# Set-up of a graph-attention kernel folded into the engines' order tables, the f2 column turned on TensorE, and a new order of all steps

## The reference

```
h  = relu(layernorm(x));  Wh = h @ W[h]                     # 4 heads, 256 -> 256
f1 = Wh . a[h, :256];  f2 = Wh . a[h, 256:]
e  = leaky(f1[n] + f2[m]), masked by adj;  attn = softmax(e)
head = elu(attn @ Wh)                                       # 4 heads side by side: 1024
out  = elu(one more such attention, W_out 1024 -> 256)      # the "BACK" head
y    = relu(out @ w1 + b1) @ w2 + b2 + out
x    = x + layernorm(y) * gamma + beta
g    = relu(layernorm(x)); Wi, Wj = halves of W
x    = x + deg * (g @ Wi.T + b) + adj @ (g @ Wj.T)
```

## Time and profile before

| | |
|---|---|
| median of 3 runs | 1505.46 us |
| the profiled execution | 1505.55 us |
| its span in the trace | 1503.5 us |
| TensorE busy | 1339.4 us, 89% |
| VectorE busy | 1190.4 us, 79% |
| ScalarE busy | 1083.5 us, 72% |
| GpSimd busy | 349.2 us, 23% |
| mean granted TensorE clock | 0.982 |

### The profile page before, as it was taken

One profiled execution on the slowest core, in us unless ns is written; L12 is line 12 of the kernel. 1 busy time (PEld: TensorE's weight loads), 2 busy tenths in 40 slices (PEclk: granted clock), 3 DMA queues, 4 the chain that ended last, 5 costly groups with the idle time before them and its releaser, 6 DMA issues.

```text
span 1503.5 us, 27090 instructions
## 1 busy us (share of the span) xinstructions
PE 1339.4 (89%) x9944; PEld 1260.0 (84%) x9944; DVE 1190.4 (79%) x2833; ACT 1083.5 (72%) x2037; POOL 349.2 (23%) x234
## 2 busy tenths in 40 slices
PE   1679898999999999999999999999999999998873
PEld 1579898888999888899988888898898999888753
DVE  6687879797988979797887979789797978968442
ACT  1577978787868778777877877687787778678431
POOL 0012123232231322223131223213122321403121
PEclk9889999999999999999999999999999999999996
DMA  4101111111101111110111111001121101101001
GB/s 169 55 22 29 22 32 34 29 36 27 50 18 29 50 29 36 37 43 15 29 50 29 47 32 36 15 29 50 29 50 29 36 15 32 34 15 36 22 20 36
DMA packets 53091, 54.07 MB, mean 36 GB/s; under 512 B 14048, under 2 KB 41696, under 8 KB 52832
## 3 DMA queue, kind: packets, MB, share of 16 engines
q1 hardware_dynamic: 52960, 52.35, 12.9%
HBM read 43.78 MB, written 8.55 MB: 35 GB/s over the span
## 4 chain that ended last, share of the span: by engine, by line
PE 51%; DVE 35%; issue 6%; ACT 5%; POOL 2%; DMA 2%; POOLq 0%; ACTq 0%; DVEq 0%; SPq 0%
PE ps L747 33%; DVE arg L625 12%; PE ps L780 5%; DVE prob_lo L606 4%; DVE arg L653 4%; PE ps L830 4%; PE ps L871 4%; PE ps L840 3%; DVE elu L661 2%; DVE zneg L633 2%; DVE whx_lo L606 2%; DVE st L587 1%; POOL hx_lo L378 1%; DVE xb L699 1%; PE ps L849 1%
## 5 line engine op out<-in xcount | busy, mean ns | idle before, releaser
L378 POOL TENSOR_TENSOR hx_lo<-elu,hx_hi 128x512 fp32r<-128x512 f32 x128 | 171.2, 1338 | 622.7 <-ACT hx_hi L474 622.7
L747 PE MATMUL ps<-prob_hi,whx_hi 128*128 128x256 f32 x1024 | 298.5, 291 | 11.4 <-DVE wk L661 7.6
L747 PE MATMUL ps<-prob_lo,whx_hi 128*128 128x256 f32 x1024 | 289.7, 283 | 0.0
L747 PE MATMUL ps<-prob_hi,whx_lo 128*128 128x256 f32 x1024 | 289.2, 282 | 0.0
L625 DVE CUSTOM_DVE_ANT_0 arg<-f2bc,mask 128x512 f32<-128x512 f32 x320 | 278.7, 907 | 1.9 <-DMA f2bc<-f_rows 1.6
L444 ACT ACTIVATE arg<-arg,nmax 128x512 f32<-128x512 f32 x320 | 227.7, 718 | 0.6 <-DVE nmax L636 0.5
L440 ACT ACTIVATE arg<-arg,fcol 128x512 f32<-128x512 f32 x320 | 213.5, 721 | 12.1 <-DVE gmax L625 12.1
L780 PE MATMUL ps<-ident,arg 128*128 128x128 f32 x1280 | 186.9, 290 | 36.9 <-DVE arg L653 32.4
L747 PEld LDWEIGHTS ps<-prob_hi,whx_hi 128*128 128x128 f32 x1024 | 196.1, 192 | 17.2 <-issue 9.7
L780 PEld LDWEIGHTS ps<-ident,arg 128*128 128x128 f32 x1280 | 170.6, 209 | 45.0 <-DVE arg L653 34.8
L450 ACT ACTIVATE prob_hi<-ps 128x1024 fp32r<-128x1024 f32 x160 | 163.4, 1021 | 58.7 <-PE ps L747 33.1
(11 more groups left out here) (126 smaller groups left out, 3142.6 us busy)
## 6 DMA issues: line engine op xcount, KB each, us to landing
f2bc<-f_rows SPq DMA_DIRECT2D x80, 256.0 KB, 3.8
xin<-in_x SPq DMA_DIRECT2D x16, 512.0 KB, 4.6
xb<-in_x SPq DMA_DIRECT2D x16, 512.0 KB, 5.0
out_x<-xb SPq DMA_DIRECT2D x16, 512.0 KB, 3.2
f_rows<-fcol SPq DMA_DIRECT2D x80, 2.0 KB, 3.4
arg<-in_adj SPq DMA_DIRECT2D x1, 1024.0 KB, 5.4
ff<-in_L_gnn_a_heads SPq DMA_DIRECT2D x1, 1024.0 KB, 9.7
ff<-in_L_gnn_W_out SPq DMA_DIRECT2D x1, 1024.0 KB, 5.6
```

The lines of the kernel that those rows point to most:

```text
L378: pool.tensor_tensor(out=hx[1][:, 2 * c.h:2 * c.h + 2, c.u * HN:(c.u + 1) * HN], in0=elu[:, c.buf, :, :], in1=hx[0][:, 2 * c.h:2 * c.h + 2 ...
L747: i = pe.matmul(out, a, b_, start=(k == 0), stop=(k == n - 1))
```

## The change

1. **Set-up in the tables.** The waits on `s_setup` and `s_hi` go. New steps are done once, for batch 0, in the tables: `wh_prep` (one head each: four dots, the split), `mask`, `gc_turn`, `wo_prep`, `adj_cast` (adj to float, deg), `adj_turn` (two chunks each), `load_wo`, `load_adj`. Each consumer has its own wait (`s_wh`, `s_mask`, `s_wo`, `s_gc_lo`, `s_adj_out`), at batch 0 only.
2. **Load order.** SP issues x of batch 0 first, then W_heads, a_heads, adj, W_gc and the rest. adj is loaded twice: once into `arg` for the mask, once more into `ff` when W_out has been used.
3. **f2 turned by TensorE.** A new step `f2turn`, five per batch: TensorE transposes the 128x4 column to 4x128 in a PSUM pair, ScalarE copies it to `f2row`, and `f2send` writes 4 pieces of 512 bytes in place of 128 of 16. The row in DRAM is then in natural order, and so are the mask and `turn_p`.
4. **New tables** for all five engines. Of TensorE 48 entries for 40 (five `f2turn`, three once-only).

The core of the diff:

```diff
+            sp.dma_start(xin[:, :, :], x_v[0]).then_inc(x_loaded, 16)
             for k in range(KC):
                 sp.dma_start(w_heads[k][:, :, :], W_heads[:, k * P:(k + 1) * P, :].rearrange("h p o -> p h o")).then_inc(ld[LD_WH], 16)
...
-                sp.dma_start(f2_rows[head % 4].rearrange("(q c) -> q c", c=NC), column, allow_slow_non_contiguous=True).then_inc(f2_out[head % 4], 16)
+                sp.wait_ge(f2_row, head + 1)
+                sp.dma_start(f2_rows[head % 4].rearrange("(c q) -> c q", c=NC), f2row[:, :]).then_inc(f2_out[head % 4], 16)
...
+            def f2row_(c):                                   # ScalarE
+                head = unit_number[c.b, c.info, 0] // 2
+                act.wait_ge(f2_turned, head + 1)
+                if head > 0:
+                    act.wait_ge(f2_out[(head - 1) % 4], 16 * ((head - 1) // 4 + 1))
+                act.activation(f2row[:, :], pairs[c.pair][0:NC, 0, 0:P], ACT.Copy).then_inc(f2_row, 1)
...
+            def wh_prep(c):                                  # VectorE
+                h = c.info
+                dve.wait_ge(ld[LD_WH], 16 * KC)
+                dve.wait_ge(ld[LD_A], 16)
+                for k in range(KC):
+                    for z in range(2):
+                        i = dot(w_heads[k][:, h, :], a_h[:, h, z, :], wsum[:, k, h, z:z + 1], 2 * k + z)
+                link(i)
+                link(dve.tensor_copy(wh[0][:, :, h, F:FA], wsum[:, :, h, :]))
+                dve.wait_ge(s_wh_hi, h + 1)
+                dve.tensor_tensor(out=wh[1][:, :, h, F:FA], in0=wsum[:, :, h, :], in1=wh[0][:, :, h, F:FA].bitcast(fp32), op=ALU.subtract)
+                for k in range(KC):
+                    i = dve.tensor_tensor(out=wh[1][:, k, h, 0:F], in0=w_heads[k][:, h, :], in1=wh[0][:, k, h, 0:F].bitcast(fp32), op=ALU.subtract)
+                i.then_inc(s_wh, 1)
...
-            pe.wait_ge(s_setup, 1)
+            pe.wait_ge(s_const, 1)
...
+            def f2turn(c):                                   # TensorE
+                h = c.info
+                head = unit_number[c.b, h, 0] // 2
+                if h == BACK:
+                    pe.wait_ge(m2_read, 2 * (c.b + 1))
+                    column = fcol2[:, 1, :]
+                else:
+                    pe.wait_ge(m1_read, 2 * H * c.b + 2 * h + 2)
+                    column = fcol[:, h, 1, :]
+                take(c.pair)
+                pe.transpose(pairs[c.pair][0:NC, 0, 0:P], column, ident[:, :]).then_inc(f2_turned, 1)
+                lend((c.pair,), (f2_row, head + 1))
...
-                        i = pe.transpose(p[:, j, n, :], arg[:, c.abuf, n, :].rearrange("p (q c) -> p c q", c=NC)[:, j, :], ident[:, :])
+                        i = pe.transpose(p[:, j, n, :], arg[:, c.abuf, n, j * P:(j + 1) * P], ident[:, :])
```

More of the change, by code:

```diff
@@ L20 @@
+    ("m1", (1, 0), 1), ("f2turn", 0, 1), ("attend", 5, 3), ("adj_turn", 0, 2), ("conv", 0, 4), ("attend", 6, 2),
+    ("turn_out", 0, 3), ("turn_p", 7, 2), ("m1", (1, 1), 1), ("turn_p", 8, 2), ("ffn1", 0, 3), ("attend", 7, 2),
[3 rows of a table added]
+    ("m1", (3, 1), 1), ("turn_p", 2, 1), ("f2turn", 2, 1), ("attend", 1, 1), ("turn_in", 0, 0), ("turn_gc", 0, 3),
+    ("attend", 2, 1), ("f2turn", 3, 1), ("turn_p", 3, 1), ("conv_in", 0, 3), ("m1", (0, 0), 0), ("turn_p", 4, 2),
 ]
 ACT_STEPS = [
-    ("probs", 4, 3), ("norm_ff_out", 0, 4), ("elu_neg", 3, 2), ("hx", 2, 2), ("elu_exp", 3, 2), ("probs", 5, 3),
@@ L23 @@
[L23 to L32, removed]
+    ("hx", 0, 3), ("probs", 2, 3), ("f2turn", 2, 3), ("elu_neg", 1, 3), ("elu_exp", 1, 3), ("turn_in", 0, 2),
@@ new lines @@
+    ("elu_exp", 6, 3), ("turn_out", 0, 4), ("probs", 7, 3), ("hx", 6, 3), ("m1", (1, 1), 2), ("probs", 8, 3), ("args", 9, 3),
+    ("ffn1", 0, 4), ("elu_neg", 7, 3), ("elu_exp", 7, 3), ("hx", 7, 3), ("elu_neg", 8, 3), ("gc_turn", 0, 2),
+    ("elu_exp", 8, 3), ("probs", 9, 3), ("f2turn", 1, 2), ("args", 0, 2), ("m1", (2, 0), 2), ("hx", 8, 3), ("args", 1, 2),
+    ("elu_neg", 9, 3), ("elu_exp", 9, 3), ("m1", (2, 1), 2), ("probs", 0, 2), ("hx", 9, 3), ("wo_prep", 0, 2),
+    ("norm_ff_out", 0, 4), ("norm_in_out", 0, 1), ("args", 2, 2), ("mix2", 0, 3), ("args", 3, 2), ("mix2", 1, 3),
@@ L33 @@
+    ("m1", (3, 0), 2), ("f2turn", -1, 3), ("probs", 1, 2), ("wh_prep", 1, 0), ("norm_gc_out", 0, 4), ("elu_neg", 0, 2),
+    ("elu_exp", 0, 2), ("m1", (3, 1), 2), ("wh_prep", 3, 1),
 ]
 DVE_STEPS = [
-    ("m1", (1, 1), 3), ("elu_out", 5, 5), ("probs", 7, 4), ("rinv", 9, 4), ("scale", 9, 4), ("elu_out", 6, 4),
-    ("probs", 8, 4), ("m1", (2, 0), 3), ("elu_out", 7, 4), ("m1", (2, 1), 3), ("rowmax", 0, 3), ("probs", 9, 4),
-    ("elu_out", 8, 4), ("rowmath", 0, 3), ("norm_gc", 0, 6), ("rowmax", 1, 3), ("rowmath", 1, 3), ("rowmax", 2, 3),
@@ L38 @@
[L38 to L47, removed]
@@ new lines @@
+    ("rinv", 9, 4), ("scale", 9, 4), ("elu_out", 7, 4), ("rowmax", 0, 3), ("elu_out", 8, 4), ("rowmath", 0, 3),
+    ("gc_turn", 0, 3), ("probs", 9, 4), ("rowmax", 1, 3), ("rowmath", 1, 3), ("rinv", 0, 3), ("norm_in_out", 0, 2),
+    ("scale", 0, 3), ("ffn2", 0, 5), ("m1", (2, 0), 3), ("norm_ff", 0, 5), ("adj_turn", 1, 4), ("rowmax", 2, 3),
+    ("rowmath", 2, 3), ("elu_out", 9, 4), ("rowmax", 3, 3), ("norm_ff_out", 0, 5), ("rinv", 1, 3), ("m1", (2, 1), 3),
+    ("scale", 1, 3), ("probs", 0, 3), ("x2", 0, 5), ("rowmath", 3, 3), ("mix2", 0, 4), ("wh_prep", 0, 2), ("norm_gc", 0, 5),
@@ new lines @@
+    ("wo_prep", 0, 3), ("mix2", 1, 4), ("rinv", 2, 3), ("norm_gc_out", 0, 5), ("m1", (3, 0), 3), ("scale", 2, 3),
+    ("probs", 1, 3), ("elu_out", 0, 3), ("rinv", 3, 3), ("scale", 3, 3), ("m1", (3, 1), 3), ("probs", 2, 3),
+    ("rowmax", 4, 4), ("rowmath", 4, 4), ("adj_cast", 0, 3), ("elu_out", 1, 3), ("turn_in", 0, 2), ("turn_gc", 0, 5),
+    ("rowmax", 5, 4), ("rinv", 4, 4), ("rowmath", 5, 4), ("scale", 4, 4), ("elu_out", 2, 3), ("rowmax", 6, 3),
+    ("probs", 3, 3), ("rowmath", 6, 3), ("wh_prep", 1, 2), ("rinv", 5, 4), ("scale", 5, 4), ("conv_in", 0, 5),
@@ L235, in gnn_kernel @@
                       "elu_out", "hx", "hx_lo")
-        IN_PSUM = ("turn_in", "m1", "turn_p", "attend", "mix2", "turn_out", "ffn1", "ffn2", "turn_gc", "conv_in", "conv")
+        IN_PSUM = ("turn_in", "m1", "f2turn", "turn_p", "attend", "mix2", "turn_out", "ffn1", "ffn2", "turn_gc", "conv_in", "conv", "gc_turn", "adj_turn")
         STEPS = {"SP": SP_STEPS, "PE": PE_STEPS, "ACT": ACT_STEPS, "DVE": DVE_STEPS, "POOL": POOL_STEPS}
@@ L253, in gnn_kernel @@
             pass
+        ONCE = ("load_wo", "load_adj", "wh_prep", "mask", "gc_turn", "wo_prep", "adj_cast", "adj_turn")
         def steps(table):
```

295 lines of the change are left out of this document (160 added, 135 removed), and 6 rows, old and new, of tables (PE_STEPS, SP_STEPS).

## The result

The changed kernel takes 1413.14 us (median of 4 runs, 1412.22 to 1413.84), the kernel before 1505.8 on the same chip (1504.39 to 1509.4). The ratio is 0.938, 95% interval 0.936 to 0.940: 6.2% faster. The forecast was 1466 us, with a range of 1443 to 1496; the gain between the two profiled executions is 92 us where 39 were expected.

A forecast was written before the change was run, and what follows sets the result against it. TensorE's instruction stream was taken as the bound in the middle: 81.9 us work plus 3.4 idle make a round of 85.3. 1505.55 - 25 (rounds) - 14 (set-up) = 1466.5, said as 1466 us, range 1443 to 1496.

The forecast's parts named there:

- Set-up: First 120 us: less VectorE idle, gain 14 us (lower end 5); first product near 18 us, first rowmax near 40.
- Turns in natural order: TensorE's turn_p: 0.10 us saved per unit, 1.0 us per round, 16 us in all.
- f2turn: 80 added TensorE transposes: 0.6 us of work a round; f2turn -1, after mix2 3, found 1.1 us late.
- Rival D: TensorE's weight loads: stepped loads held back more, 56 ns for each of 1280, 72 us in place of 16: 1410; chance 0.03.
- TensorE's work: Steady rounds: 82.3 - 1.0 + 0.6 = 81.9 us of TensorE work a round.
- New order, VectorE: Steady rounds: rowmax slower than priced, some 0.4 us missed at half a dozen places, 2.3 of 3.4 us idle a round.
- Start and end: First 120 us: 14 us gained; last 104 us: 0 counted, between 8 lost and 10 won.
- A: Steady rounds stay as they are, only the set-up's 14 us are won: 1491 us; chance 0.24.
- B: PSUM pairs become the bound at four takers, 8.8 us idle a round, kernel slower: 1545 us; chance 0.10.
- C: Steady rounds: order as good as the walk without VectorE's delays, 1.1 us idle a round: 1433 us; chance 0.13.

The follow-up runs named there:

- e8: Kernel before with only the set-up changed (set-up steps entered into the old tables, x loaded first), old order and f2 form kept: 1491.40 us, 0.988.
- e1: Changed kernel in its new order with f2turn, but the column's send in 128 pieces, mask and turn_p stepped as before: 1420.84 us, 0.940.
- e5: Kernel before with all four GpSimd instructions (hx_lo, gamma, beta, b2) on a sixteenth of their columns: 1419.59 us, 0.940.
- e14: e2 with TensorE's five f2turn entries kept as takers of a PSUM pair that turn nothing: 1411.79 us, 0.933.
- e3: Kernel before, own set-up and old order, with f2turn and natural order put in: 1560.65 us, 1.033.
- e7: Changed kernel with the old tables' order, its new steps (set-up, f2turn) put in: 1549.44 us, 1.025.
- e12: e3 with all GpSimd's long steps on a sixteenth of their columns, the edit of e5: 1496.85 us, 0.991.
- e11: Kernel before, GpSimd's gamma, beta and b2 on a sixteenth of their columns, each followed by GpSimd work on a scratch tile nobody reads: 1488.69 us, 0.985.
- e6: Changed kernel with GpSimd's long steps on a sixteenth of their columns, the edit of e5: 1383.52 us, 0.916.
- e2: Changed kernel with its new order, less f2turn and less natural order: 1398.53 us, 0.925.

## Why the prediction was wrong, point by point

- *Set-up*, 14 us: e8 gives 18, so the size was about right, partly by luck. The 14 were counted as idle time of VectorE in the first 120 us, 31.8 less 17 (its terms as written add up to 16.2) less 1.2. Measured are 120 - 97.95 = 22.1 us idle, by which the same sum would give 8.5, while TensorE's busy time there rose by 17.7. The first product starts at 16.30 (forecast about 18), the first `rowmax` at 35.86 (near 40), in the kernel after:

```profile
4.85 1.40 DVE L634 BATCH_NORM_STATS2 st<-xin 128x6 f32<-128x256 f32 x4 [4.85 <-DMA xin<-in_x]
...
35.86 0.69 DVE L675 CUSTOM_DVE_ANT_0 arg<-f2bc,mask 128x512 f32<-128x512 f32 x1
```
```profile
16.30 0.55 PE L781 MATMUL ps<-wh_hi,hT_hi 128*128 128x258 f32 x1 [2.46 <-DVE hT_lo L652]
```

- *Turns in natural order*, 0.10 us a unit, 16 us: the size of the turn was right (0.88 to 0.79 us in the timelines, the median from the first transpose to the next step), what it is worth was not. In e1 and after, TensorE's work falls from 81.9 to 81.1 us a round, nearly the 1.0 said, but its idle grows from 1.0 to 1.4: 3 to 8 us remain. Rival D, 56 ns for each of 1280, is refuted: the loads became 67 ns shorter, the kernel at most 8 us.
- *f2turn*, 0.6 us of work a round and 1.1 of idle by the late `f2turn` -1: the sum, 1.7, is close to the 1.61 measured (81.22 to 82.83), but for another reason. `f2turn` has no wait in the steady rounds; most of the idle comes from the rotation, at `conv` (5.3 of e1's 7.0 us in the middle). I had counted the 43 takers, and searched for the shortest distances only next to `attend`.
- *TensorE's work*, 81.9 us a round: 0.8 too high. e5 shows the flaw: with no gap left, a round with the old steps takes 80.75 us, though I had read 82.3 us of work in it. The busy time of the earlier trace rows contained some 1.5 us a round that go when the waits go. Part of it is that the record of a matmul behind idle time is longer, 362 ns at the mean for 45 of them in the middle, against 295 for all: 0.4 us a round. Where the rest lies stays open.
- *New order, VectorE*: **here the prediction failed.** It said that `rowmax`'s mean is 0.91 us, "stretched beside GpSimd's instructions", and took the stretch for a property of the kernel that would stay in the new order, at a price of 2.3 us idle a round. Measured are 684 ns and 1.39 us idle a round for all causes, where I had 3.4. Of the 1.39, 0.87 are the wait at `conv` that the pairs' rotation brought (e14) and 0.57 one for a pair that `conv_in` had; the 1.1 at `f2turn` -1 didn't come. So whatever VectorE's delays still cost, it was 1.4 at most and not 2.3. The stretch was a hold that depends on what starts beside what, so on the order itself. The two rows that would have told it (the 2.88 us `rowmax` and GpSimd's addition beside it) were in the trace before. Less idle (2.0 us) and less work (0.8) together make the round 2.8 us shorter than forecast, 41 of the 53 us of the error, 30 of them the idle.
- *Start and end*: TensorE's busy time of the first 120 us rose by 17.7 us where 14 were counted, that of the last 104 by 4.4 where I had 0. That is 8 of the remaining 12 us; the other 4 are not located.
- *Rivals.* A and B are refuted in the new order; B's mechanism is real and cost 13 us (e14). In the old order f2turn does make the kernel slower than before (e3, e7), and e12's first wait is for a pair, but taking the pairs alone was not tried there. C had the right direction and nearly the right idle (1.1 us for 1.39), and still gave 1433: its 81.9 us of work a round are 12 us too many, the start and the end another 8.

That the new order wins *because* of the holds is shown in this form: the old order loses 91 us to GpSimd's width, at least 45 of them to pure occupation (e11), the new one 29.6 (e6), the held `rowmax` are gone from its trace, and with GpSimd narrow the two orders' rounds differ by 0.12 us. `hx_lo`'s own width, 24 of the 91 us, and the 22 us that e11 didn't bring back can be holds or earlier results. How much of the 93 us of e8 to e2 would be left in an order of the same table with the holds restored was not tried.

## What to carry to other kernels

Where one instruction form has a mean well above its fastest, look at its longest ones beside the other engines before pricing an order: if they end a fixed time after another engine's instruction (here 0.55 us, 24 times of 24), it is a hold, and moving one or the other removes it whole. Beside a long GpSimd instruction put VectorE work with an operand in PSUM, or start the VectorE instruction first. And price a new small step on TensorE by the buffer that it takes from a rotation: here that was 13 of 22 us, its own transposes 5.
